# Inverse norms of queries and keys: a power on GpSimd in place of logarithm, exponential and a Newton step on ScalarE and VectorE

## The reference, cut to what matters

```python
def l2norm(t):
    return t / jnp.clip(jnp.linalg.norm(t, axis=-1, keepdims=True), 1e-12)

h = shift_token(x); qkv = h @ wqkv
q, k, v = jnp.split(qkv, 3, axis=-1)          # then split into 8 heads
q = l2norm(q) * qs
k = l2norm(k) * ksc
q, k = rotary_xpos(q, k)
o = local_attention(q, k, v)                  # softmax((q * 8.0) @ k^T), window 64
```

## The kernel before

| slot | TensorE | ScalarE | VectorE | GpSimd |
|---|---|---|---|---|
| Q0 | qk of k=0, first values | squares 0 | rotated 0 | added 0 |
| Q1 | values, qk of k=1 | rescale 0, squares 1 | square_sums 0, rotated 1 | added 1 |
| Q2 | values, turn queries 0 | rescale 1 | refined 0, square_sums 1 | normed_keys 0 |
| Q3 | turn queries 1, turn keys 0 | copies | refined 1 | normed_keys 1 |
| Q4 | turn keys 1 | copies | | |

## Time and profile before

### The profile page before, as it was taken

The page is one execution under the profiler, slowest core; times in us unless marked ns, Lnnn a source line. Parts: engine busy times, 40 slices in busy tenths (PEclk is TensorE's granted clock), DMA queues, the critical chain, the costliest instruction groups (busy, mean ns, idle before and its releaser), DMA issues. The chain is left out here.

```text
span 1631.8 us, 26756 instructions
## 1 busy us (share of the span) xinstructions
PE 1309.1 (80%) x10226; PEld 881.1 (54%) x10226; DVE 816.4 (50%) x2202; ACT 900.7 (55%) x2266; POOL 459.9 (28%) x596
## 2 busy tenths in 40 slices
PE   4677888779787887877988798787798888887786
PEld 4455555447565564544665555554575556454465
DVE  2453555636444537456356355455456552744633
ACT  1333557466564366744884355654676435664485
POOL 0331334212234233230034333421015423423002
PEclk9977798999797989979999799799999798898999
DMA  7102000000012100000001110000001210000000
GB/s 255 39 22 57 18 5 1 1 4 1 8 43 65 22 13 1 1 1 5 1 24 46 51 26 5 1 1 1 5 7 46 63 29 6 1 1 1 1 1 7
DMA packets 41854, 36.02 MB, mean 22 GB/s; under 512 B 31296, under 2 KB 35904, under 8 KB 40192
## 3 DMA queue, kind: packets, MB, share of 16 engines
q1 hardware_dynamic: 41728, 34.33, 7.1%
HBM read 25.30 MB, written 7.44 MB: 20 GB/s over the span
## 5 line engine op out<-in xcount | busy, mean ns | idle before, releaser
L1033 ACT ACTIVATE arena<-ps 128x512 f32<-128x512 f32 (+6 forms) x560 | 260.5, 498 | 323.1 <-PE ps L539 40.8
L1747 POOL TENSOR_TENSOR arena<-arena,small 128x512 f32<-128x512 f32 x96 | 99.8, 1039 | 241.2 <-DVE small L1365 240.8
L1778 POOL TENSOR_TENSOR arena<-arena 128x512 f32<-128x512 f32 x64 | 81.2, 1270 | 302.2 <-DVE arena L1387 302.0
L1369 DVE TENSOR_REDUCE small<-ps 128x4 f32<-128x512 f32 (+3 forms) x96 | 83.2, 867 | 158.2 <-PE ps L567 87.5
L1230 ACT ACTIVATE arena<-ps,small 128x192 f32<-128x192 f32 (+1 forms) x256 | 121.0, 492 | 40.3 <-DVE small L1555 40.3
L578 PE MATMUL ps<-packed,arena 128*128 128x128 f32 x384 | 77.7, 336 | 37.6 <-POOL arena L1747 15.0
L1603 DVE TENSOR_REDUCE small<-ps 128x4 f32<-128x1024 f32 x64 | 75.4, 1219 | 41.3 <-PE ps L918 41.0
L1504 DVE TENSOR_TENSOR gath<-ps,rank_tab 96x512 f32<-96x512 f32 x96 | 63.6, 684 | 51.0 <-PE ps L527 50.6
L708 PE MATMUL ps<-w_experts,arena 128*128 128x128 f32 x544 | 70.4, 281 | 17.1 <-DVE arena L1656 10.2
L578 PEld LDWEIGHTS ps<-packed,arena 128*128 128x128 f32 x384 | 50.6, 168 | 59.4 <-POOL arena L1747 18.8
L1656 DVE TENSOR_TENSOR arena<-arena,ps 128x512 f32<-128x512 f32 x64 | 42.2, 685 | 80.2 <-ACT arena L1321 63.3
(11 more groups left out here) (288 smaller groups left out, 3068.3 us busy)
## 6 DMA issues: line engine op xcount, KB each, us to landing
idxb<-idx_scratch SPq DMA_DIRECT2D x8, 1536.0 KB, 6.3
score_scratch<-arena SPq DMA_DIRECT2D x24, 256.0 KB
w_experts<-in_experts SPq DMA_DIRECT2D x3, 1088.0 KB, 14.8
w_wqkv<-in_wqkv SPq DMA_DIRECT2D x1, 1536.0 KB, 9.1
arena<-score_scratch SPq DMA_DIRECT2D x96, 16.0 KB, 2.0
arena<-arena SPq DMA_DIRECT2D x96, 16.0 KB, 1.8
arena<-in_x SPq DMA_DIRECT2D x8, 128.0 KB, 2.2
out_x<-arena SPq DMA_DIRECT2D x8, 128.0 KB, 1.9
```

The costliest lines, as they stand in the source:

```text
L1033: return act.activation(dst, src, ACT.Copy)
L1369: st.link(dve.tensor_reduce(mx[s][:, u, :].rearrange("p (i j) -> p i j", j=2), src, AX.X, ALU.max))
L1747: ins = pool.tensor_tensor(part, part, bc(rl[s][:, u, :], 2, P), ALU.mult)
L1778: ins = pool.tensor_tensor(own, own, turned, ALU.add)
```

## The change

The logarithm and the exponential on ScalarE (`rescale`), the Newton step on VectorE (`refined`) and the floor on VectorE go. `normed_keys` on GpSimd waits for the sums of squares, puts the floor on them itself and raises them to the power -1/2, both on 128x16, each linked; then comes the product as before. The scale of 8 is put into the query part of the rotation table, on the host, so `cqs` goes too and its readers take `rs`. A column `minus_half` of 128x1 takes the place of `shift_col`.

```diff
-LN_SHIFT = 65536.0
+QK_SCALE = 8.0
...
-    x = np.stack([np.cos(fr) * sc, np.cos(fr) / sc, np.sin(fr) * sc * sign, np.sin(fr) / sc * sign], 1)
+    x = np.stack([QK_SCALE * np.cos(fr) * sc, np.cos(fr) / sc, QK_SCALE * np.sin(fr) * sc * sign, np.sin(fr) / sc * sign], 1)
...
-            def rescale(l, k):
-                act.wait_ge(*at("ssq_ready", 2 * l + k + 1))
-                st.link(act.activation(rs[s][:, k, :], ssq[s][:, k, :], ACT.Ln, scale=LN_SHIFT))
-                act.activation(rs[s][:, k, :], rs[s][:, k, :], ACT.Exp, scale=-0.5, bias=shift_col[:, :]).then_inc(*one("rs_ready"))
...
                     values_out(l, 1)
-                    rescale(l, 0)
                     squares(l, 1)
...
                     queries_turned(l, 0, 3)
-                    rescale(l, 1)
...
-                                                     ACT.Exp, bias=nb[s][:, i, h:h + 1], scale=cqs[s][:, T, hh_:hh_ + 1],
+                                                     ACT.Exp, bias=nb[s][:, i, h:h + 1], scale=rs[s][:, T, hh_:hh_ + 1],
...
-                st.link(dve.tensor_reduce(ssq[s][:, k, :], m.squares[k].rearrange("p (h n) -> p h n", n=DH), AX.X, ALU.add))
-                dve.tensor_scalar(ssq[s][:, k, :], ssq[s][:, k, :], 1e-24, None, ALU.max).then_inc(*one("ssq_ready"))
-
-            def refined(l, k):
-                dve.wait_ge(*at("rs_ready", 2 * l + k + 1))
-                nt, g = newton[s], rs[s][:, k, :]
-                st.link(dve.tensor_tensor(nt, ssq[s][:, k, :], g, ALU.mult))
-                st.link(dve.scalar_tensor_tensor(nt, nt, -0.5, g, ALU.mult, ALU.mult))
-                st.link(dve.scalar_tensor_tensor(g, nt, 1.5, g, ALU.add, ALU.mult))
-                dve.tensor_scalar(cqs[s][:, k, :], g[:, 0:H], 8.0, None, ALU.mult).then_inc(*one("rs_final"))
+                dve.tensor_reduce(ssq[s][:, k, :], m.squares[k].rearrange("p (h n) -> p h n", n=DH), AX.X, ALU.add)\
+                   .then_inc(*one("ssq_ready"))
...
                     yield f"Q1.{l}"
-                    refined(l, 0)
                     square_sums(l, 1)
                     yield f"Q2.{l}"
-                    refined(l, 1)
...
-            dve.memset(shift_col[:, :], 0.5 * math.log(LN_SHIFT)).then_inc(sig("cols_set"), 1)
+            st.mark(dve.memset(minus_half[:, :], -0.5))
...
             def normed_keys(l, k):
-                pool.wait_ge(*at("rs_final", 2 * l + k + 1))
+                pool.wait_ge(*at("ssq_ready", 2 * l + k + 1))
+                st.link(pool.tensor_scalar(ssq[s][:, k, :], ssq[s][:, k, :], 1e-24, None, ALU.max))
+                st.link(pool.tensor_tensor(rs[s][:, k, :], ssq[s][:, k, :], minus_half[:, :].broadcast_to([P, 2 * H]), ALU.pow))
                 own = m.own[k][:, 512:].rearrange("p (h n) -> p h n", h=H)
                 pool.tensor_tensor(own, own, bc(rs[s][:, k, H:], 2, DH), ALU.mult).then_inc(*one("k_ready"))
```

More of the change, by code:

```diff
@@ L141 @@
     "qkv_mm": ["qk_mm", "qk_mm", "v_mm", "v_mm", "qk_mm", "qk_mm", "v_mm", "q_turn", "q_turn", "k_turn", "k_turn"] * 2,
-    "qkv_act": ["qk_squared", "qk_squared", "v_copied", "v_copied", "rs_ready", "qk_squared", "qk_squared", "v_copied",
-                "q_copied", "rs_ready", "q_copied", "k_copied", "k_copied"] * 2,
-    "qkv_dve": ["qk_parts", "qk_parts", "ssq_ready", "qk_parts", "qk_parts", "rs_final", "ssq_ready", "rs_final"] * 2,
+    "qkv_act": ["qk_squared", "qk_squared", "v_copied", "v_copied", "qk_squared", "qk_squared", "v_copied",
+                "q_copied", "q_copied", "k_copied", "k_copied"] * 2,
+    "qkv_dve": ["qk_parts", "qk_parts", "ssq_ready", "qk_parts", "qk_parts", "ssq_ready"] * 2,
     "qkv_pool": ["q_added", "q_added", "k_ready", "k_ready"] * 2,
@@ L382, in program @@
         one_col = sb("one_col", [P, 1])
-        shift_col = sb("shift_col", [P, 1])
+        minus_half = sb("minus_half", [P, 1])
         modT = sb("modT", [P, 12, B])
@@ L394, in program @@
         ssq, rs = ([t[:, 64 + 32 * i:96 + 32 * i].rearrange("p (k n) -> p k n", k=NT) for t in small] for i in range(2))
-        cqs = [t[:, 128:144].rearrange("p (k n) -> p k n", k=NT) for t in small]
-        newton = [t[:, 144:160] for t in small]
         mx1 = [t[:, 160:192].rearrange("p (k n) -> p k n", k=NT) for t in small]
@@ L1329, in _ @@
             act.wait_ge(sig("weights_loaded"), 16 * (len(loads) + len(rows)))
-            act.wait_ge(sig("cols_set"), 4)
+            act.wait_ge(sig("cols_set"), 3)
             act.activation(c_den[:, :, :], cT[:, :, :], ACT.Exp, scale=-1.0).then_inc(sig("setup_exp"), 1)
@@ L1554, in vector_stream @@
                             maxima(i, keys(i // 2))
-                            dve.scalar_tensor_tensor(nb[s][:, i, :], mx[s][:, i, :], -1.0, cqs[s][:, i // 2, 4 * (i % 2):4 * (i % 2) + 4],
+                            dve.scalar_tensor_tensor(nb[s][:, i, :], mx[s][:, i, :], -1.0, rs[s][:, i // 2, 4 * (i % 2):4 * (i % 2) + 4],
                                                      ALU.mult, ALU.mult).then_inc(*one("u_bias"))
@@ L1681, in _ @@
                 dve.tensor_scalar(t[:, 4, :], t[:, 3, :], 0.5, None, ALU.mult).then_inc(sig("delta_ready"), 1)
-            dve.wait_ge(sig("cols_set"), 4)
+            dve.wait_ge(sig("cols_set"), 3)
             st.mark(dve.tensor_tensor(center_mat[:, :], ident, mean_mat[:, :], ALU.subtract))
```

## The result

The changed kernel takes 1698.4 us in the median (1682.0 to 1699.3, 4 runs) against 1634.3 us of the kernel before in the same series: a ratio of 1.037, 95% interval 1.028 to 1.046, some 61 us slower (46 to 75). The span of the profiled execution grew from 1631.8 to 1697.4 us, by 65.6.

The account below looks back on a forecast made before the run. TensorE was taken to wait at the end of the norm chain through GpSimd's key products. 32 x 1.4 - 45.8 = -1.0 us on the median of 1629.9 gave 1629 us, range 1603 to 1683.

Parts of the forecast that it names:

- the chain: Sums, floor, logarithm, exponential, Newton step, key product, turning of the keys: the path TensorE waits behind, 42.8 us.
- a cheap power: Rival: GpSimd's power takes under 0.5 us, kernel 1603 to 1613 us, TensorE's key wait near 20; chance 0.25.
- the 42.8 us of waiting: TensorE's idleness at the turning of the keys for GpSimd's key product, in 26 places.
- The second sums come early enough: VectorE's second sums of squares, no longer behind the first Newton step, are done before GpSimd asks, at all three places.
- 4x - 6.45: Change in us at a round's second place (two layers, four key products), from first adds' end to last product.
- x: Time of floor and power with their links on GpSimd ahead of each key product; taken as 1.4 us.
- 32x - 45.8 us: Change of the whole kernel, four rounds of three places each; pays under 1.43 us, forecast -1.0 us.
- x = p + 0.40: GpSimd's time ahead of each key product: the power's duration p plus 0.40 us for floor and links.
- p = 1.0 us: Duration of one GpSimd power on 128x16, guessed from some 30 passes at the plain column rate.
- the third one: Slow power rival: GpSimd's power takes 1.53 to about 4 us and holds everything up; +16 to +95 us, chance 0.26.
- unoverlapped passes: Within the slow-power rival: each pass of GpSimd's power costs twice the row's rate, power 1.81 us, kernel 1655 us.
- What I left at nothing: Power catching VectorE's bias, at most +4 us; TensorE starting slowly behind longer waits, at most +6 us.

Follow-up runs that it names:

- e1: The changed kernel with a plain GpSimd product of 128x16 in place of the power; 1610.0 us, ratio 0.985 to the kernel before.
- e3: The kernel before without its Newton step, with the factor 8 in the rotation table; 1594.2 us, ratio 0.9765 to the kernel before.
- e2: The changed kernel with the power carried out twice in a row; 1787.6 us, ratio 1.0945 to the kernel before.
- e6: The changed kernel with six linked two-input VectorE instructions on a scratch tile added in each layer; longest of 96 took 0.68 us, kernel time not asked.
- e9: The changed kernel with eighteen linked two-input VectorE instructions on a scratch tile laid over the power; the group takes 3.93 us, kernel time not asked.
- e7: The kernel before with the first half's Newton step moved on VectorE to where GpSimd has no add; 1621.5 us, ratio 0.9925.
- e5: The changed kernel with its power of 16 columns split into two of 8, each linked; 1710.8 us in one execution.
- e8: The kernel before without Newton step and without VectorE's floor, 1e-24 added as the logarithm's bias instead; 1594.6 us, ratio 0.974 to the kernel before.

## Why the prediction was wrong

**What bounds the kernel, and the chain.** Right: TensorE waits at the end of this chain, and each microsecond on it counts in full. The wait at L667 grew by 58.6 us. The forecast of the wait itself for a cheap power, "near 20 if the power is cheap", was off: 34.3 in e1. So was the sentence that the 42.8 us of waiting are "nearly all that a shorter chain can give back". No kernel here measurably gained more than that, but in e3 only 23.5 us of the gain came out of this wait; TensorE's own busy time gave 24.5.

**The second sums come early enough, and GpSimd sets the pace.** Right for the changed kernel. The floor waited for VectorE for 0.2 us in all, and GpSimd worked with hardly a gap behind the adds. 4x - 6.45 was 7.0 against 7.3 measured. In e1, where x is small, it holds less well: the floor waited 3.0 us for VectorE, and adds waited too.

**32x - 45.8 us.** The slope is right, 31.6 measured against 32, and so is the time at each x: 0.67 gives -24, measured -24; 3.37 gives +62, measured +61 by the ratio and +65.6 by the spans; 6.34 gives +157, measured +155; and the kernel without Newton step at the near end, -38 measured against -44 at most for x = 0.05. That it fits to a few microseconds is in part luck. The second round does not stand for all four, because the third place of the first round did not grow. In the traces the twelve stretches from the adds to the last product changed by -41.1 us (e3), -21.5 (e1), +56.9 (changed kernel) and +151.2 (e2), the spans by -39.0, -25.2, +65.6 and +150.8. In the changed kernel the sum has 5 us too much in the stretches and nothing for the 9 us that came outside them.

**x = p + 0.40.** Right to 0.03 us: 2.94 + 0.40 = 3.34, measured 3.37. The floor took 253 ns, not 210.

**p = 1.0 us.** This is the step that failed: "Some 30 passes (my count for two polynomials with their splitting and joining, an estimate) make 0.80 us and p = 1.01". The power took 2.94 us, 1.94 more than I took, and 32 x 1.94 = 62 is the whole miss. The split shows where: 0.16 us a column, where 30 passes at the plain rate are 0.05. Which steps a power is made of, and how many, no run shows; the 30 had nothing in the traces behind them. I had priced an arithmetic that I had only imagined by the throughput of a long streaming operation, and had put the middle of the chances on it. The case that came is the third one, "p from 1.53 to about 4", which had 0.26. The range stopped at p = 2.7, inside that case: 1683, where 1698 was measured. A bound drawn through the middle of a rival whose price no row shows was a bound on nothing. The rival's own value with unoverlapped passes, 1.81 us, points the right way and is still 1.1 us short.
**What I left at nothing.** The catching of VectorE's two-input instructions by the power does not happen (e6, e9). The slower TensorE is there: the clock at the second place fell from 0.95 to 0.78 over the same work, and over the whole span from 0.90 to 0.885, with 15.8 us more of TensorE busy for the same matmuls, where I had allowed 6 at most. The rows that I took for it don't show a start that is slow behind a long wait: the turning of 0.66 us stood behind a wait of 2.06 and the one of 1.12 behind 2.04. The wait for the product and the busy time together grew by 74.4 us and the span by 65.6, so TensorE's other idle time shrank by 9. What the lower clock alone costs no run separates.

**The stall as a rule.** The rule of the Trainium skill, page SBUF — State Buffer, section Who interferes with whom, that such a VectorE instruction and a GpSimd instruction that reads SBUF shut each other out, held for the add: 19 executions of L1399 ended some 30 ns behind an add, and where the Newton step was moved away from the adds 15 of the 19 stalls went (e7). It did not hold for the power, which reads SBUF too: 208 two-input instructions ran inside powers in e9, none longer than 203 ns. Here the measurement decides.

## What to carry to other kernels

An operation that no row of the trace shows deserves a measurement of its duration before it is put on a chain that every engine waits for; the chain's arithmetic can be right to a few microseconds, as here, and the forecast is still only as good as this one number. The same arithmetic says what it may cost at the most: here 1.43 us for floor and power together, against 3.37. Where a small instruction of VectorE shows a median seven times its minimum, look for the GpSimd instruction above it; and ask whether a refinement is needed at all before asking where to compute it, which here was worth 38 us, at the price of its precision.

## What the runs showed of the hardware that was not expected

- A power on GpSimd takes 2.94 us on 128x16 and 1.65 us on 128x8 (e5): 0.16 us a column, against 1.67 ns of a product (rows 5).
- Its duration hardly varied with the data that it met here: 2924 to 3051 ns over the 32 executions of the changed kernel.
- It does not hold off VectorE instructions with two SBUF inputs (208 inside powers, none over 203 ns, e9), while an add on GpSimd does, for up to 1.1 us (1268 ns against 174, rows 4).
- A logarithm on ScalarE with a column as its bias takes 306 ns on 128x16 (e8), without one 216 (rows 3); the exponential with a column took 308 all along.
